# Conv gate and attention on one core: late value groups, early second sigmoids, and the last block's sums on other engines

## The chip, the cores and the metric

One core of a Trainium2 chip runs the whole program. The metric is the device time of one execution in microseconds (us), median of three runs. The core has TensorE (matmuls into PSUM), VectorE, ScalarE, GpSimd (which doesn't reach PSUM here) and SyncE, which issues the DMAs. Each engine works through its own queue in order; semaphores tie the queues together. In the profile they are PE (and PEld for its weight loads), DVE, ACT, POOL and SP.

## The reference

```python
# x: (2, 64, 96, 96); for each of the two images:
h = group_norm1(x, n1_g, n1_b)                    # over the whole image
f = dwconv(h, w3, b3) + dwconv(h, w5, b5) + dwconv(h, w7, b7)
g = sigmoid(conv1x1(f, gate_w, gate_b))
x = x + conv1x1(f * g, proj_w, proj_b)
h = group_norm1(x, n2_g, n2_b)
q, k, v = 1x1 convolutions of h, as (N=9216, 64), (64, N), (N, 64)
attn = softmax(q @ k / 8)                          # 9216 x 9216
out = x + (attn @ v) as an image
```

## The kernel before

**Tiling.** An image's 64 channels x 9216 pixels lie as 128 partitions (two halves of the image) x 4608 columns, in 9 chunks of 512 columns (`CH`). Attention runs in 18 blocks (`NBLK`) of 512 queries; a block visits 36 pairs (`NPAIR`) of key groups of 128. For each pair TensorE makes the scores (`scores`, L969), ScalarE takes the exponential into one of 8 slots of `E` (L538), GpSimd adds one half of it to `accA` (`add_a`, L468) and VectorE the other half to a PSUM bank (`add_b`, L792), and TensorE multiplies it with the values into the accumulation bank (`weigh`, L978). In between TensorE and VectorE look for the row maxima of the next block (`max_scores`, L985, and `reduce_max`, L776). The maxima, once complete, are combined (`maxima`, L783), widened by ScalarE (`widen_maxima`, L561), spread by TensorE (`spread_maxima`, L994) and placed by ScalarE among the queries (`place_maxima`, L567). From the fourth pair on, every odd pair has its scores "seeded": ScalarE copies the maxima into the banks first (`seed`, L574).

**A block's end.** VectorE copies its half of the row sums out of PSUM (`sums_out`, L799), GpSimd adds both parts to `accS` (`total`, L482), TensorE sums over partitions with a matrix of ones (`row_sums`, L1001), ScalarE copies these (`copy_row_sums`, L554), VectorE takes 8 reciprocals of 32 columns (`reciprocals`, L808). The value sums come out of PSUM in four copies (`move_pv`, L547), are added (L501 on GpSimd, or `sum_pv`, L820, on VectorE), multiplied with the reciprocals (L505 or `normalize`, L825), and `write_out` (L833) adds bias and residual. For 17 of an image's 18 blocks this happens during the next block. For an image's last block it is done at once: ScalarE moves all value sums and the row sums right after its last exponential, VectorE takes reciprocals, sum, normalization and write-out right after `sums_out`.

**The seam between the images.** For each of the 9 chunks of the next image TensorE makes the gate product (L1113), ScalarE the sigmoid into `gs` (L628), GpSimd multiplies it with `f` (L511), TensorE makes the projection (L1128), VectorE adds it to x (L891) and takes statistics (`x1_stats`, L883). TensorE issues gate 0, gate 1, the row sums of the last block, and then for each chunk c gate c+2 and projection c. `gs` lies in slots 2 and 3 of `E`, so ScalarE waits ahead of the first sigmoid of image 1 until all additions of the last block are done. After chunk 8 come the aggregate (L898) and a chain of small operations, and SP issues the block's output stores (L400) and, later, the first queries.

**The start of an image's attention.** The list `ITEMS` has 27 entries: 18 chunks of q and k (products L1172, evacuated twice by ScalarE at L653 and L655, with the low part on GpSimd, L521), then 9 groups of values (8 matmul records each, L1163, evacuated at L646). The items use three PSUM banks in turn. From the fourth item on (`LOOK = 3`) the 36 looks (`NVIS`) for block 0's maxima are placed between them: `looks_after(i)` says which looks follow item i, spread evenly over the 24 items left. VectorE reduces each. Then the maxima are widened, spread and placed, and block 0 starts.

Of the kernel before, what the change touches and what calls it, by code (L numbers as in the profile page):

```python
# [9 lines left out]
ALU = mybir.AluOpType  # L10
# [54 lines left out]
def program(nc, x, x_rows, conv_w, per_row, per_channel, matrices, matrices_t, out):  # L65
    with ExitStack() as ctx:
# [96 lines left out]

        ps = ctx.enter_context(nc.psum_tensor("ps", [P, 8, CH], F32))
        S_BANK, MX_BANK, ACC_BANK, SUM_BANK = 0, 4, 6, 7
        STAT_BANK = 3
        STAT1_BANK = (7, 3)
        PROJ_BANK = 2
# [83 lines left out]

        ITEMS = QK_CHUNKS + [(2, g) for g in range(NCH)]
        LOOK = 3
        ITEM_BANK = (2, 3, 6)
        FIRST_MX = (0, 4)

        def looks_after(i):
            each = len(ITEMS) - LOOK
            return range(max(0, i - LOOK) * NVIS // each, max(0, i + 1 - LOOK) * NVIS // each)  # L260

# [165 lines left out]
        def _(pool):  # L429
# [77 lines left out]
            for b in range(B):  # L507
                for c in range(NCH):
                    pool.wait_ge(sig_ready, NCH * b + c + 1)
                    at = f[:, c * CH:(c + 1) * CH]  # L510
                    nc.gpsimd.tensor_tensor(at, at, gs[:, c % 3, :], ALU.mult).then_inc(fg_ready, 1)  # L511
                pool.wait_ge(spread_ready, b + 1)
                nc.gpsimd.partition_all_reduce(reach[:], spread[:], P, RMAX).then_inc(reach_ready, 1)

                for c, (which, chunk) in enumerate(QK_CHUNKS):
                    n = 2 * NCH * b + c
                    cols = slice(chunk * CH, (chunk + 1) * CH)
                    hi, lo = ((QH, QL), (KH, KL))[which]
                    pool.wait_ge(t_ready, n + 1)
                    pool.wait_ge(hi_ready, n + 1)  # L520
                    nc.gpsimd.tensor_tensor(lo[:, cols], T[:, c % 4, :], hi[:, cols], ALU.subtract).then_inc(lo_ready, 1)  # L521
                for j in range(NBLK):
                    attend(b, j)
                total(blk(b, NBLK - 1))


        @block.scalar
        def _(act):
# [89 lines left out]
            for b in range(B):  # L618
                if b:

                    act.wait_ge(adda_free, NSLOT + pair0(b, 0))
                    act.wait_ge(addb_free, NSLOT + pair0(b, 0))
                for c in range(NCH):
                    n = NCH * b + c
                    act.wait_ge(gate_ready, n + 1)
                    if c >= 3:
                        act.wait_ge(fg_ready, n - 2)
                    nc.scalar.activation(gs[:, c % 3, :], ps[:, c % 2, :], ACT.Sigmoid,  # L628
                                         bias=prm[:, GB:GB + 1]).then_inc(sig_ready, 1)
                if b == 0:  # L630
                    act.wait_ge(conv_ps, BESIDE + 1)
                    act.wait_ge(f_out[BESIDE % 2], 16 * COLS * (BESIDE // 2))
                    nc.scalar.activation(evac[:, BESIDE % 2, :, :], ps[:, 4:8, 0:WN], ACT.Copy).then_inc(conv_out, 1)
# [7 lines left out]
                act.wait_ge(scale_ready, b + 1)  # L641
                for i, (which, chunk) in enumerate(ITEMS):
                    bank = ITEM_BANK[i % 3]
                    if which == 2:
                        act.wait_ge(v_ps, NCH * b + chunk + 1)
                        nc.scalar.activation(vals[:, chunk * CH:(chunk + 1) * CH], ps[:, bank, :], ACT.Copy).then_inc(v_out, 1)  # L646
                    else:
# [3 lines left out]
                        if n >= 4:  # L651
# [2 lines left out]
                                             bias=plus, scale=by).then_inc(hi_ready, 1)  # L654
                        nc.scalar.activation(T[:, i % 4, :], ps[:, bank, :], ACT.Identity,  # L655
                                             bias=plus, scale=by).then_inc(t_ready, 1)
                widen_maxima(blk(b, 0))
                place_maxima(blk(b, 0))
                for j in range(NBLK):
                    attend(b, j)  # L660
                move_pv(blk(b, NBLK - 1))
                copy_row_sums(blk(b, NBLK - 1), MX_BANK + 1)


        @block.vector
        def _(dve):
# [211 lines left out]
            for b in range(B):  # L878
# [6 lines left out]
                for c in range(NCH):  # L885
                    n = NCH * b + c
                    dve.wait_ge(proj_ready, n + 1)
                    if c == 0:
                        dve.wait_ge(x_ready, 32 * (b + 1))
                    at = x1[:, c * CH:(c + 1) * CH]  # L890
                    nc.vector.scalar_tensor_tensor(out=at, in0=ps[:, PROJ_BANK + c % 2, :], scalar=prm[:, PB:PB + 1],  # L891
                                                   in1=xs[:, c * CH:(c + 1) * CH], op0=ALU.add,
                                                   op1=ALU.add).then_inc(x1_ready, 1)
                    if c:
                        x1_stats(c - 1)
                x1_stats(NCH - 1)
                dve.wait_ge(bn_done, NCH * (b + 1))
                nc.vector.bn_aggr(mv[:], flat(bn[:])).then_inc(st_in, 1)  # L898
# [34 lines left out]
                maxima(blk(b, 0))  # L933
                for j in range(NBLK):
                    attend(b, j)
                n = blk(b, NBLK - 1)
                for k in range(RECS):
                    reciprocals(n, k)
                sum_pv(n)
                normalize(n)  # L940
                write_out(b, NBLK - 1)


        @block.tensor
        def _(pe):
# [43 lines left out]
            def spread_maxima(n):  # L989

                pe.wait_ge(nm_ready, n + 1)
                for q in range(NQT):
                    for h in (0, 1):
                        a = nc.tensor.matmul(ps[C * h:C * h + C, S_BANK, q * P:(q + 1) * P], negm[:, q, 0:C], ident16[:],  # L994
                                             start=True, stop=True)
                a.then_inc(mb_ready, 1)

            def row_sums(n, bank):
                pe.wait_ge(sum_ready, n + 1)
# [106 lines left out]
            for b in range(B):  # L1106
# [80 lines left out]
                attend(b, NCH - 2, 1)  # L1187
                attend(b, NCH - 1, 0, looks=1)
                attend(b, NCH - 1, 1, looks=0)
            row_sums(B * NBLK - 1, MX_BANK + 1)  # L1190


# [45 lines left out]
```

## Time and profile before

| | us |
|---|---|
| median of three runs | 2831.35 (2830.12 to 2832.53) |
| the profiled execution | 2830.9 |
| its span in the trace | 2828.9 |
| PE busy | 2763.1 (98%) |
| DVE busy | 2503.6 (89%) |
| ACT busy | 2208.5 (78%) |
| POOL busy | 1823.9 (64%) |

The difference between execution and span, 2.0 us, lies around the traced work. Image 0's attention runs from about 164 to 1453 us of the span, image 1's from about 1531 to 2820. A busy share is an average over the stages; at the seam, at the start of an attention and at the end of the program the shares are lower than these. Times in rows are in us from the span's start.

### The profile page before, as it was taken

What the parts mean: (1) busy time and instruction counts of PE and PEld (TensorE: products, weight loads), DVE (VectorE), ACT (ScalarE), POOL (GpSimd) and SP (SyncE); (2) the same over time, 40 slices, a digit from 0 to 9 for tenths busy, and PEclk for the clock granted to TensorE, in tenths of its full rate; (3) what the DMA queues carried; (4) which work ended last, traced back from release to release, by engine and by line L of the source; (5) the groups of instructions that cost most, each with busy time, mean ns of one, the idle gap of its engine ahead of it and who ended that gap; (6) DMA issues with size and microseconds to landing.
All of it is one profiled execution on the core that took longest, in us unless ns stands there. A gap on an engine that the chain in (4) does not pass through costs nothing.

```text
span 2828.9 us, 54483 instructions
## 1 busy us (share of the span) xinstructions
PE 2763.1 (98%) x19644; PEld 935.7 (33%) x19644; DVE 2503.6 (89%) x3172; ACT 2208.5 (78%) x2291; POOL 1823.9 (64%) x1479
## 2 busy tenths in 40 slices
PE   7889999999999999999988999999999999999998
PEld 4233333333333333333323333333333333333332
DVE  5589999999999999999758999999999999999984
ACT  4467888888888888888866788888888888888887
POOL 1446666666666666666754666666666666666666
PEclk9999999999999999999999999999999999999999
DMA  6103000000000000000000000000000000000000
GB/s 203 40 9 75 10 11 10 11 10 10 11 10 11 10 11 11 10 11 9 5 5 16 9 10 11 10 11 11 11 10 10 11 10 11 11 10 11 9 5 5
DMA packets 35768, 48.20 MB, mean 17 GB/s; under 512 B 7848, under 2 KB 33960, under 8 KB 34992
## 3 DMA queue, kind: packets, MB, share of 16 engines
q1 hardware_dynamic: 35504, 44.75, 6.0%
q8 instruction: 157, 2.57, 0.4%
q14 instruction: 107, 0.88, 0.1%
HBM read 16.41 MB, written 9.44 MB: 9 GB/s over the span
## 4 chain that ended last, share of the span: by engine, by line
PE 93%; DVE 4%; issue 1%; ACT 1%; POOL 0%; SPq 0%; DMA 0%; POOLq 0%; DVEq 0%; ACTq 0%
PE ps L978 42%; PE ps L969 35%; PE ps L985 12%; DVE mxp L776 3%; PE ps L1086 2%; PE ps L1113 1%; PE ps L1001 1%; PE ps L1128 0%; DVE ps L792 0%; PE ps L1172 0%; PE ps L1062 0%; PE ps L994 0%; ACT arena L538 0%; DVE bn L883 0%; ACT ps L574 0%
## 5 line engine op out<-in xcount | busy, mean ns | idle before, releaser
L468 POOL TENSOR_TENSOR arena<-arena 128x512 f32<-128x512 f32 x1224 | 1558.8, 1273 | 792.6 <-ACT arena L538 713.7
L776 DVE TENSOR_REDUCE mxp<-ps 128x1 f32<-128x1024 f32 x1296 | 1575.7, 1220 | 174.5 <-PE ps L985 142.6
L538 ACT ACTIVATE arena<-ps,bnd 128x1024 f32<-128x1024 f32 x1296 | 1373.0, 1110 | 422.0 <-PE ps L969 371.7
L978 PE MATMUL ps<-arena,vals 128*64 128x512 f32 x5184 | 1268.2, 605 | 0.2
L969 PE MATMUL ps<-arena 64*128 64x512 f16 x7776 | 1055.1, 377 | 4.1 <-ACT ps L574 2.3
L792 DVE TENSOR_TENSOR ps<-ps,arena 128x512 f32<-128x512 f32 x1224 | 844.8, 690 | 68.1 <-ACT arena L538 67.3
L574 ACT ACTIVATE ps<-mseed 128x1024 f32<-128x1024 f32 x612 | 629.0, 1028 | 53.1 <-ACT arena L538 0.4
L969 PEld LDWEIGHTS ps<-arena 64*128 64x128 f16 x7776 | 376.5, 94 | 419.8 <-ACT arena L538 27.6
L985 PE MATMUL ps<-arena,QM 64*128 64x512 f16 x2592 | 500.6, 383 | 14.1 <-DVE mxp L776 9.6
L978 PEld LDWEIGHTS ps<-arena,vals 128*64 128x64 f32 x5184 | 310.8, 136 | 501.6 <-issue 337.9
L985 PEld LDWEIGHTS ps<-arena,QM 64*128 64x128 f16 x2592 | 124.7, 93 | 734.1 <-DVE mxp L776 632.4
L969 PE MATMUL ps<-arena,one 64*128 64x512 f16 x1368 | 260.9, 378 | 0.0
L808 DVE RECIPROCAL rec<-rsum 128x32 f32<-128x32 f32 x288 | 96.9, 340 | 6.6 <-ACT rsum L554 6.5
L969 PEld LDWEIGHTS ps<-arena,one 64*128 64x128 f16 x1368 | 67.0, 94 | 81.6 <-issue 1.2
L487 POOL TENSOR_SCALAR mseed<-arena 128x512 f32<-128x512 f16 x36 | 53.6, 1490 | 37.3 <-ACT arena L567 34.4
L473 POOL TENSOR_TENSOR arena<-arena 128x512 f32<-128x512 f32 x36 | 45.9, 1275 | 37.8 <-ACT arena L538 37.8
L1086 PE MATMUL ps<-arena 32*24 32x384 f32 x1792 | 54.5, 529 | 13.6 <-issue 7.6
L521 POOL TENSOR_TENSOR arena<-arena 128x512 f16<-128x512 f32 x36 | 41.4, 1159 | 31.8 <-ACT arena L655 31.8
L1172 PE MATMUL ps<-f,wT 128*128 128x512 f32 x72 | 42.4, 685 | 4.9 <-ACT f L639 3.2
L628 ACT ACTIVATE arena<-ps,prm 128x512 f32<-128x512 f32 x18 | 12.3, 687 | 44.6 <-PE ps L1113 44.6
L482 POOL TENSOR_TENSOR accS<-arena 128x512 f32<-128x512 f32 x36 | 46.6, 1295 | 0.2
L511 POOL TENSOR_TENSOR f<-f,arena 128x512 f32<-128x512 f32 x18 | 23.1, 1287 | 36.3 <-ACT arena L628 36.3
(116 smaller groups left out, 668.8 us busy)
## 6 DMA issues: line engine op xcount, KB each, us to landing
arena<-arena SPq DMA_DIRECT2D x144, 64.0 KB, 2.0
arena<-in_x_rows SPq DMA_DIRECT2D x8, 816.0 KB, 10.2
xs<-in_x SPq DMA_DIRECT2D x4, 1152.0 KB, 16.3
f_scratch<-arena SPq DMA_DIRECT2D x32, 144.0 KB
f<-f_scratch SPq DMA_DIRECT2D x16, 288.0 KB, 9.5
QM<-arena SPq DMA_DIRECT2D x72, 64.0 KB, 2.0
xst<-arena SPq DMA_DIRECT2D x72, 64.0 KB, 1.9
out<-ot SPq DMA_DIRECT2D x72, 64.0 KB, 2.0
```

The lines of the kernel that those rows point to most:

```text
L468: nc.gpsimd.tensor_tensor(accA[:, n % 2, :], accA[:, n % 2, :], e, ALU.add).then_inc(adda_free, 1)
L482: nc.gpsimd.tensor_tensor(accS[:], accA[:, n % 2, :], accB[:], ALU.add).then_inc(sum_ready, 1)
L487: nc.gpsimd.tensor_scalar(mseed[:, n % 2, :], QS[:, n % 2, 2, :], ONE * C, None, ALU.mult).then_inc(mseed_ready, 1)
L538: nc.scalar.activation(flat(E[:, slot_of(n % 2, p), :, :]), flat(ps[:, S_BANK + 2 * buf:S_BANK + 2 * buf + 2, :]), ACT.Exp, scale=bnd[:, 6 ...
L574: nc.scalar.activation(ps[:, S_BANK + 2:S_BANK + 4, :], mseed[:, n % 2, :].unsqueeze(1).to_broadcast([P, 2, CH]), ACT.Copy).then_inc(seede ...
L776: nc.vector.reduce_max(flat(mxp[:])[:, v:v + 1], flat(ps[:, bank:bank + 2, :]), AX.X).then_inc(mx_free, 1)
L792: nc.vector.tensor_tensor(ps[:, SUM_BANK, :], ps[:, SUM_BANK, :], e, ALU.add).then_inc(addb_free, 1)
L808: nc.vector.reciprocal(rec[:, at], rsum[:, at]).then_inc(rec_ready, 1)
L969: a = nc.tensor.matmul(ps[:, S_BANK + 2 * (p % 2) + t, :], of[rows], QS[rows, par, part, :], start=(k == 0 and seeds is None), stop=(k == ...
L978: a = nc.tensor.matmul(ps[C * t:C * t + C, ACC_BANK, :], V[:, p, t, :], E[:, slot_of(par, p), t, :], start=(p == 0), stop=(p == NPAIR - 1) ...
L985: a = nc.tensor.matmul(ps[:, bank + t, :], QM[rows, half, qt * P:(qt + 1) * P], KH[rows, kc * CH:(kc + 1) * CH], start=True, stop=True)
L1086: a = nc.tensor.matmul(ps[GRP * h:GRP * h + WROWS, conv_bank(s) + g, 0:WN].rearrange("p (w x) -> p w x", x=W), bands[rows, k * KW + dx, :] ...
```

## The change

It has three parts.

1. **Late value groups.** `looks_after` spreads the 36 looks over items 3 to 24 instead of 3 to 26. The last two value groups come after the last look, with none behind them (`LATE = 2`). ScalarE widens the maxima before it evacuates the last value group, not after it. This is done in both images.
2. **Early second sigmoids.** In image 1, ScalarE waits ahead of the first sigmoid only for the additions up to the last four pairs (`GS_PAIRS`), whose slots `gs` doesn't use. The copies of the last block of image 0 move in between the sigmoids: two value-sum copies each after chunks 1 and 2, the row-sum copy after chunk 3. On VectorE its reciprocals move behind chunks 4 and 5, sum and normalization behind chunk 6, the write-out behind chunk 7.
3. **The program's last block.** GpSimd no longer adds `accA` and `accB`; TensorE sums both over partitions into the same PSUM columns (`row_sums_of_parts`). VectorE takes one reciprocal of 256 columns straight from PSUM; ScalarE's copy goes. GpSimd adds the value sums instead of VectorE.

```diff
@@ looks @@
+        LATE = 2
         def looks_after(i):
-            each = len(ITEMS) - LOOK
-            return range(max(0, i - LOOK) * NVIS // each, max(0, i + 1 - LOOK) * NVIS // each)
+            each = len(ITEMS) - LOOK - LATE
+            return range(min(max(0, i - LOOK), each) * NVIS // each, min(max(0, i + 1 - LOOK), each) * NVIS // each)
@@ gpsimd, after an image's blocks @@
-                total(blk(b, NBLK - 1))
+                n = blk(b, NBLK - 1)
+                if b + 1 < B:
+                    total(n)
+                else:
+                    pool.wait_ge(acc_free, 4 * (n + 1))
+                    pool.wait_ge(o_ready, n + 1)
+                    nc.gpsimd.tensor_tensor(pvt[:], pva[:], pvb[:], ALU.add).then_inc(pv_summed, 1)
@@ scalar @@
-                    act.wait_ge(adda_free, NSLOT + pair0(b, 0))
-                    act.wait_ge(addb_free, NSLOT + pair0(b, 0))
+                    act.wait_ge(adda_free, NSLOT + pair0(b, 0) - GS_PAIRS)
+                    act.wait_ge(addb_free, NSLOT + pair0(b, 0) - GS_PAIRS)
                 for c in range(NCH):
...
+                    if b and c in (1, 2):
+                        move_pv(blk(b, 0) - 1, ((c - 1, 0), (c - 1, 1)))
+                    if b and c == 3:
+                        copy_row_sums(blk(b, 0) - 1, MX_BANK + 1)
...
                 for i, (which, chunk) in enumerate(ITEMS):
                     bank = ITEM_BANK[i % 3]
+                    if i == len(ITEMS) - 1:
+                        widen_maxima(blk(b, 0))
...
-                widen_maxima(blk(b, 0))
                 place_maxima(blk(b, 0))
                 for j in range(NBLK):
                     attend(b, j)
-                move_pv(blk(b, NBLK - 1))
-                copy_row_sums(blk(b, NBLK - 1), MX_BANK + 1)
+                if b + 1 == B:
+                    move_pv(blk(b, NBLK - 1))
@@ vector @@
+                    if b and c in (4, 5):
+                        for k in range(RECS // 2 * (c - 4), RECS // 2 * (c - 3)):
+                            reciprocals(blk(b, 0) - 1, k)
+                    if b and c == 6:
+                        sum_pv(blk(b, 0) - 1)
+                        normalize(blk(b, 0) - 1)
+                    if b and c == 7:
+                        write_out(b - 1, NBLK - 1)
...
-                n = blk(b, NBLK - 1)
-                for k in range(RECS):
-                    reciprocals(n, k)
-                sum_pv(n)
-                normalize(n)
-                write_out(b, NBLK - 1)
+            n = blk(B - 1, NBLK - 1)
+            dve.wait_ge(rs_ready, n + 1)
+            dve.wait_ge(norm_done, n)
+            nc.vector.reciprocal(rec[:], ps[:, MX_BANK + 1, 0:HCH]).then_inc(rec_ready, RECS)
+            normalize(n)
+            write_out(B - 1, NBLK - 1)
@@ tensor @@
+            def row_sums_of_parts(n, bank):
+                pe.wait_ge(accb_out, n + 1)
+                for h in (0, 1):
+                    nc.tensor.matmul(ps[C * h:C * h + C, bank, 0:HCH], ones[:, 0:C],
+                                     accB[:, h * HCH:(h + 1) * HCH], start=True, stop=False)
+                pe.wait_ge(adda_free, NSLOT + NPAIR * (n + 1))
+                for h in (0, 1):
+                    a = nc.tensor.matmul(ps[C * h:C * h + C, bank, 0:HCH], ones[:, 0:C],
+                                         accA[:, n % 2, h * HCH:(h + 1) * HCH], start=False, stop=True)
+                a.then_inc(rs_ready, 1)
...
-            row_sums(B * NBLK - 1, MX_BANK + 1)
+            row_sums_of_parts(B * NBLK - 1, MX_BANK + 1)
```

## Rows read from the trace of the kernel before

**Rows 1.** The page, part 4: the chain that ended last, shares by engine.
```profile
PE 93%; DVE 4%; issue 1%; ACT 1%; POOL 0%; SPq 0%; DMA 0%; POOLq 0%; DVEq 0%; ACTq 0%
```

**Rows 2.** By stretches: length, busy us (count) of five engines, granted clock, DMA.
```profile
1458.40:1462.00 3.60, 3.58 (x5) 1.46 (x6) 2.85 (x3) 1.23 (x2) 3.51 (x3) 0.53 0.00 0
1510.00:1528.00 18.00, 16.25 (x106) 10.47 (x104) 17.99 (x17) 7.44 (x12) 2.82 (x3) 1.00 0.06 15
1528.00:1534.00 6.00, 3.07 (x22) 1.40 (x24) 1.29 (x2) 3.19 (x4) 1.54 (x1) 0.69 0.17 44
```

**Rows 3.** Timeline, seam: start, duration, engine, line, operation, [idle before <-releaser].
```profile
1453.37 1.98 PE L1113 MATMUL ps<-f,wT 128*128 128x512 f32 x4
...
1455.29 0.65 PE L1001 MATMUL ps<-accS,ones 128*64 128x256 f32 x4
...
1458.67 1.32 DVE L825 TENSOR_TENSOR pvt<-pvt,rec 128x256 f32<-128x256 f32 x1
...
1463.65 1.02 PE L1113 MATMUL ps<-f,wT 128*128 128x512 f32 x2
...
1465.48 1.26 POOL L511 TENSOR_TENSOR f<-f,arena 128x512 f32<-128x512 f32 x1 [0.44 <-ACT arena L628]
...
1469.01 0.75 DVE L891 SCALAR_TENSOR_TENSOR arena<-ps,prm,xs 128x512 f32<-128x512 f32 x1 [0.36 <-PE ps L1128]
...
1470.52 1.02 PE L1113 MATMUL ps<-f,wT 128*128 128x512 f32 x2
...
1473.71 0.73 DVE L891 SCALAR_TENSOR_TENSOR arena<-ps,prm,xs 128x512 f32<-128x512 f32 x1
...
1474.96 0.73 DVE L891 SCALAR_TENSOR_TENSOR arena<-ps,prm,xs 128x512 f32<-128x512 f32 x1
...
1476.92 0.40 DVE L898 BATCH_NORM_AGGREGATE mv<-bn 128x2 f32<-128x54 f32 x1
```

**Rows 4.** Timelines of DVE, PE and ACT, start of image 1's attention.
```profile
1487.89 41.21 DVE L776 TENSOR_REDUCE mxp<-ps 128x1 f32<-128x1024 f32 x36 [2.99 <-PE ps L985]
...
1525.22 1.16 PE L1163 MATMUL ps<-wT,f 128*128 128x128 f32 x8
...
1529.36 0.63 ACT L561 ACTIVATE negm<-m 128x512 f16<-128x512 f32 x1 [2.35 <-DVE m L783]
...
1530.04 0.45 PE L994 MATMUL ps<-ident,negm 128*64 128x128 f16 x8 [2.86 <-ACT negm L561]
...
1531.15 1.28 ACT L538 ACT_TABLE_LOAD   x1
...
1535.02 1.11 ACT L538 ACTIVATE arena<-ps,bnd 128x1024 f32<-128x1024 f32 x1 [0.59 <-PE ps L969]
...
1536.22 1.03 ACT L574 ACTIVATE ps<-mseed 128x1024 f32<-128x1024 f32 x1
...
1537.40 0.82 PE L969 MATMUL ps<-arena 64*128 64x512 f16 x6 [0.28 <-ACT ps L574]
```

**Rows 5.** Timelines of ACT and PE, start of image 0's attention.
```profile
163.80 0.60 ACT L567 ACTIVATE arena<-ps 128x512 f16<-128x512 f32 x1 [0.51 <-PE ps L994]
...
170.41 0.82 PE L969 MATMUL ps<-arena 64*128 64x512 f16 x6 [1.09 <-ACT ps L574]
```

**Rows 6.** Timeline of the program's tail.
```profile
2816.78 3.65 PE L978 MATMUL ps<-arena,vals 128*64 128x512 f32 x16
...
2821.28 0.78 ACT L547 ACTIVATE pvb<-ps 64x256 f32<-64x256 f32 x2
...
2822.69 1.83 DVE L808 RECIPROCAL rec<-rsum 128x32 f32<-128x32 f32 x8 [2.87 <-ACT rsum L554]
...
2824.91 0.43 DVE L825 TENSOR_TENSOR pvt<-pvt,rec 128x256 f32<-128x256 f32 x1
2825.37 0.48 DVE L833 SCALAR_TENSOR_TENSOR ot<-pvt,prm,xst 128x256 f32<-128x256 f32 x1
```

**Rows 7.** Instructions of L501: count, duration in ns (min/median/max), first and last start.
```profile
L501 POOL TENSOR_TENSOR pvt<-pva,pvb x34: 723/730/742, 269.4 to 2779.6; 128x256 f32<-128x256 f32 x34
```

More of the change, by code:

```diff
@@ L165, in program @@
         S_BANK, MX_BANK, ACC_BANK, SUM_BANK = 0, 4, 6, 7
+        GS_PAIRS = 4
         STAT_BANK = 3
```

## The prediction

> **What bounds the kernel now.** I first read the chain that ended last. TensorE holds 93% of it [rows 1], and in the attention blocks TensorE runs without gaps, so nothing of this change that lies beside those blocks counts. The change touches three other places, which I then read in the timeline and in the view by stretches: the seam between image 0 and image 1, the start of the first attention block of each image, and the tail after the last block. In all three TensorE waits for a serial chain through other engines. Twice the granted clock then falls to half: 0.53 in the seam's first sigmoid chunks and 0.69 on average around the start of block 0 [rows 2].
>
> **Seam, what sets its length.** Before, ScalarE moves the value sums, waits for the row sums, copies them, loads the sigmoid table and only then starts chunk 0. Afterwards TensorE paces the chunks: gate matmuls 4 and 8 start at 1463.65 and 1470.52, so one chunk (a gate and a projection product) takes 6.87 / 4 = 1.72 us [rows 3]. VectorE ends the stage: the last x1 chunk starts at 1474.96 and the aggregate of the statistics at 1476.92 [rows 3]. That aggregate is my marker.
>
> **Seam, the change.** The wait on the last four pairs goes. Those pairs use other slots of E than the sigmoid results, and the awaited additions are done while the block still runs. The table load has to follow the last exponential. I take it that it runs ahead of the gate wait, as the exponential's load does: it starts at 1531.15, when the scores it serves aren't there yet (TensorE makes them from the placed maxima, which are finished just then) [rows 4]. Gate 0 starts at 1453.37. A gate's start is followed by its product on GpSimd 1.83 us later (1463.65 to 1465.48), which takes 1.26 [rows 3], so product 0 is ready at 1456.46. On TensorE the four row-sum passes end at 1455.29 + 0.65 = 1455.94 [rows 3]. Gate 2 follows there, and projection 0 at 1456.80, so GpSimd is in time and TensorE has no gap in which the clock falls. Gate 8 then starts at 1455.94 + 6 x 1.72 = 1466.25 instead of 1470.52: **4.27 us** earlier. Of this 1.8 is the half-clock stretch.
>
> VectorE cannot follow. Its eight reciprocals, sum, normalize and write-out stood ahead of chunk 0, in time when it had nothing else; now they stand in chunks 4 to 7, where it has 1.72 - 1.25 = 0.47 spare per chunk (1.25 from chunk 7 at 1473.71 to chunk 8 at 1474.96 [rows 3]). From chunk 4 on it is the bound. Chunk 4 started at 1469.01 [rows 3], now at 1464.74. From there come four pairs of 1.25, the last chunk's 1.96 up to the aggregate, and the moved work. The same work at the tail, with GpSimd idle, takes from 2822.69 to 2825.37 + 0.48, or 3.16 us [rows 6]. The aggregate starts at 1464.74 + 5.00 + 1.96 + 3.16 = 1474.86 against 1476.92: a gain of **2.1 us**. Half of the 4.27 is given back, since the cover is gone. ScalarE's four copies (0.39 each) and the row-sum copy fit into its slack between sigmoids. The stores of the last block are issued later by SP; it queues the first queries of image 1 behind them, but these wait for a q chunk that comes ten us after either write-out. Cost nothing. Bounds: +0.8 if the table load stood behind the gate wait (1.3 later), and -0.6 if sum, normalize and write-out all took what normalize takes beside busy GpSimd (1.32 instead of 0.43 [rows 3, 6], some 0.9 more for each of the three). I take 2.1, since the last product on GpSimd ends near 1469.4 and the sum comes only at about 1470.3.
>
> **Start of block 0.** 36 reductions run back to back on VectorE for 41.21 us up to 1529.10 [rows 4]. Spreading the looks over 22 instead of 24 items cannot shorten that, and TensorE keeps up: it is busy for 16.25 of 18 us of that stretch, VectorE for 17.99 [rows 2], and two items leave it. What changes is what TensorE does at the end. It has been idle for 2.86 us before the maxima are spread at 1530.04 [rows 4], so from 1527.18, and the clock falls. Now two value groups (1.16 each [rows 4]) stand there and end at 1529.5, before the widened maxima arrive at 1529.99 (1529.36 + 0.63). The waits that remain are 0.5 us there and some 0.9 for the placed maxima. The drop followed a wait of 2.86 us, so I take it that with these the clock stays. On ScalarE one eviction of 0.60 now stands between widening and placing; it fills a wait for TensorE and delays placing by 0.1. It also queues behind ScalarE's wait for the maxima, and only the first scores, which wait for the placing anyway, wait for it.
>
> With the full clock the chain from the placed maxima to the first seeded pass of scores belongs to ScalarE: load 1.30, two exponentials of 1.11, a gap of 0.09, the seed of 1.03, and 0.15 to TensorE, or 4.79 us [rows 4]. A warm pass (0.82 for six matmuls [rows 4]) hides in the load and in the exponential. Before, it was 1537.40 - 1531.13 = 6.27 in image 1 and 170.41 - 164.40 = 6.01 in image 0 [rows 5]. The gains are 1.48 and 1.22, less 0.1 each: **2.5 us**. Bounds: -0.2 (the clock falls all the same) and +2.8.
>
> **Tail.** Before, VectorE's part goes over GpSimd's total, four row-sum passes, ScalarE's copy, eight reciprocals and the sum to normalize at 2824.91 [rows 6]. Now the passes over accB and accA follow the last value matmul at 2816.78 + 3.65 = 2820.43; both parts are ready by then. Eight passes cost at most twice the 0.65 of four [rows 3], I take until 2821.6. One reciprocal of 256 columns isn't in the trace: bounds are 0.43 (normalize, of the same shape) and 1.83 (the eight, whose columns these are) [rows 6]; I take 1.5, near the eight, as it is their operation and only their starts are saved. Normalize can begin at 2821.6 + 0.05 + 1.5 + 0.05 = 2823.2. GpSimd's value sum starts when ScalarE's moves end at 2821.28 + 0.78 = 2822.06, takes 0.73 and is over at about 2822.9 [rows 6, 7]: hidden. Gain **1.7 us**, bounds 1.25 (2821.73 and 1.83) and 2.0 (GpSimd's sum is then last).
>
> By the Trainium skill, "VectorE: DVE Perf Modes", "First, the fixed hardware budget", the reciprocal is an iterative divide with a repeat count of 8; read as eight cycles per column at its 0.96 GHz that is an estimate of 2.13 us for 256 columns, a tail gain near 0.9 and a whole gain near 5.5. The trace is against this reading: the eight together need 1.83 with all their starts.
>
> **The sum.** 2.5 + 2.1 + 1.7 = 6.3 us. The profiled execution took 2830.9 (span 2828.9, 2.0 around it), 0.45 under the median of 2831.35; it becomes 2824.6, and the median 2825.05, so **2825.1**.
>
> **The rivals.**
> - The clock falls at block 0 although the value groups fill the wait, since two waits and the short spread still leave TensorE half idle there. For it: the drop before followed 2.86 us of waiting; against it: the new waits are under 1. Block 0 gives -0.2, the sum is 3.6, the time 2827.7. Chance 0.2.
> - VectorE's moved work meets GpSimd's products. Then the seam gives -0.6, the sum is 3.6 and the time 2827.7. For it: normalize took 1.32 beside them [rows 3]; against it: by then the products should have ended. Chance 0.12. The Trainium skill, "SBUF — State Buffer", "SBUF: two separate sides", says that a VectorE operation with two SBUF inputs and a GpSimd operation exclude each other for a whole instruction; the 1.32 agrees.
> - The sigmoids don't start early, because the table load stands behind the gate wait: the seam gives 0.8, the time is 2826.4. Chance 0.08.
> - The reciprocal is dearer than its eight parts (by the rule above the tail gives 0.9): 2825.9. Chance 0.06.
> - **Slower**: with value groups taken out from between the looks, TensorE idles more while VectorE reduces, and the clock falls already there. The two late groups then run at half speed, 2 x 2.2 = 4.4 us, to 1531.6, the spread (0.9) ends 2.0 later than before, in both images, and the start stays cold. It decides from the point where the groups end after 1530.0. Block 0 costs 4.0; with the seam's bad end (-0.6) and the tail's 1.7 the sum is 2.9 slower, 2834.2. Against it: without two groups (2.3 us) TensorE still works for some 14 of the 18 us [rows 2]. Chance 0.04.
>
> **How the numbers follow.** The forecast has 0.5, between 2823.0 and 2826.8. To hold 8 in 10, the range reaches to the two rivals at 2827.7 and their spread: 2823.0 to 2828.3. A difference of 0.2% (5.7 us, so a time under 2825.7) is about what a measurement of this kernel can tell. The forecast is only 0.6 from that border: of its 0.5 about 0.42 is beyond it, and the dearer reciprocal and the good ends of the rivals add 0.08. The slower rival's time is within 0.2% of now; only its far part is beyond. Faster 0.5, same 0.48, slower 0.02.
>
> **What would show it.** Seam: first sigmoid near 1454.4, no clock below 1.0 from 1453 to 1470, VectorE without gaps from chunk 4, aggregate near 1474.9. Block 0: the reductions still end within 0.2 us of 1529.1 less the seam's gain; 4.8 to 4.9 us from placed maxima to the seeded scores, at full clock. Tail: normalize 2.8 us after the last value matmul instead of 4.5, one reciprocal of 1.5. The forecast is wrong if the clock falls at 1530, if the moved work takes over 4 us, or if an attention block changes its pace.

## The result and the profile after

The changed kernel takes 2824.27 us (median of 14 runs, 2822.21 to 2826.88) against 2830.28 (14 runs, 2828.25 to 2832.53) of the kernel before in the same comparison: 6.0 us less, ratio 0.9979 with a 95% interval of 0.9972 to 0.9986 (a gain between 4.0 and 7.9 us). Forecast were 6.3 us less and a time of 2825.1. The profiled execution took 2825.39 with a span of 2823.7, 5.2 under the span of before.

The page of the changed kernel, busy shares and chain by engine:

```profile
span 2823.7 us, 54475 instructions
PE 2759.1 (98%) x19648; PEld 935.0 (33%) x19648; DVE 2501.6 (89%) x3164; ACT 2207.9 (78%) x2290; POOL 1823.3 (65%) x1479
PE 93%; DVE 4%; issue 1%; ACT 1%; POOL 0%; SPq 0%; DMA 0%; DVEq 0%; ACTq 0%; POOLq 0%
```

Neither the shares nor the chain [rows 1] show where 5 us went; they are spread over three places. So I cut both traces at the same instructions and compare the stretches. The numbers are differences of times in the timelines. "Gate 0" is the start of image 1's first gate product, "aggregate" that of the x1 statistics' aggregate, "first reduction" VectorE's first reduction of a look, "m4" the instruction that combines the maxima (L783), "placed" the end of `place_maxima` and "seeded" the start of the first scores on seeded banks:

| stretch (us) | before | after | gain |
|---|---|---|---|
| start to image 0's aggregate (not touched) | 105.84 | 105.17 | 0.67 |
| image 0: first reduction to m4 | 42.50 | 42.37 | 0.13 |
| image 0: placed maxima to first seeded scores | 6.01 | 4.71 | 1.30 |
| image 0: from there to gate 0 (attention) | 1282.96 | 1282.95 | 0 |
| seam: gate 0 to aggregate | 23.55 | 22.49 | 1.06 |
| seam: aggregate to first reduction | 10.97 | 12.24 | -1.27 |
| image 1: first reduction to m4 | 41.24 | 41.12 | 0.12 |
| image 1: placed maxima to first seeded scores | 6.27 | 4.72 | 1.55 |
| image 1: from there to the last value matmul's end | 1283.03 | 1283.00 | 0 |
| tail: from there to normalize | 4.48 | 2.88 | 1.60 |

The stretches not listed are the same within 0.05. Part 1 gives 3.1 us here, part 3 1.6, part 2 nothing (1.06 - 1.27 = -0.2), and 0.67 lies ahead of all changes, where this stretch took 102.1 to 106.1 in the executions profiled for this study.

**Seam.** The changed kernel's timeline, which answers to [rows 3] (start, duration, engine, line, operation, [idle before <-releaser]):

```profile
1451.28 1.98 PE L1148 MATMUL ps<-f,wT 128*128 128x512 f32 x4
...
1452.51 1.28 ACT L638 ACT_TABLE_LOAD   x1 [3.23 <-PE ps L1148]
1453.19 0.65 PE L1036 MATMUL ps<-accS,ones 128*64 128x256 f32 x4
1453.80 1.26 ACT L638 ACTIVATE arena<-ps,prm 128x512 f32<-128x512 f32 x2
1454.54 1.12 PE L1148 MATMUL ps<-f,wT 128*128 128x512 f32 x2 [0.70 <-ACT arena L638]
...
1463.92 0.75 DVE L906 SCALAR_TENSOR_TENSOR arena<-ps,prm,xs 128x512 f32<-128x512 f32 x1 [0.36 <-PE ps L1163]
...
1465.18 0.97 DVE L823 RECIPROCAL rec<-rsum 128x32 f32<-128x32 f32 x4
...
1468.93 1.10 PE L1163 MATMUL ps<-f,wT 128*128 128x512 f32 x2 [0.76 <-DVE arena L906]
1469.30 0.41 DVE L835 TENSOR_TENSOR pvt<-pva,pvb 128x256 f32<-128x256 f32 x1
...
1473.77 0.40 DVE L921 BATCH_NORM_AGGREGATE mv<-bn 128x2 f32<-128x54 f32 x1
```

The second line is the surprise. ScalarE is idle for 3.23 us and loads the table only when gate 0 is there; TensorE then waits 0.70 us for the sigmoid ahead of gate 2, up to 1454.54. From chunk 4 (1463.92) on VectorE has no gap, and TensorE waits for it ahead of the last projection (0.76). From 1453 to 1470 the clock stays at full, where it was 0.53 in the first chunks before [rows 2]. But it falls afterwards. By stretches (length, busy us and count of PE, PEld, DVE, ACT, POOL, granted clock, DMA share, GB/s):

```profile
1453.00:1470.00 17.00, 15.33 (x37) 6.03 (x36) 10.79 (x23) 9.81 (x16) 11.35 (x9) 1.00 0.00 1
1471.00:1484.00 13.00, 6.21 (x10) 3.19 (x11) 9.09 (x33) 4.62 (x8) 1.53 (x2) 0.51 0.08 20
1527.00:1534.00 7.00, 4.03 (x39) 1.70 (x39) 2.72 (x4) 6.48 (x9) 2.80 (x2) 1.00 0.11 28
```

It falls during TensorE's wait for the statistics. The first statistics product of the kernel before, and behind it that of the changed kernel:

```profile
1477.38 0.38 PE L951 MATMUL ps<-mv,ones 128*128 128x2 f32 x2 [2.59 <-DVE mv L898]
1474.22 0.59 PE L974 MATMUL ps<-mv,ones 128*128 128x2 f32 x2 [4.20 <-DVE mv L921]
```

In the kernel before the wait was 2.59 us and this product still ran at full clock; the clock fell only behind it (0.57 from 1478 to 1486). In the changed kernel the wait is 4.20 us and the product takes 0.59 instead of 0.38.

**Start of block 0** (1527 to 1534, last line): clock 1.00, where it was 0.69 [rows 2]. TensorE's timeline there, which answers to [rows 4]:

```profile
1525.21 2.05 PE L1198 MATMUL ps<-wT,f 128*128 128x128 f32 x16
1528.04 0.41 PE L1017 MATMUL ps<-ident,negm 128*64 128x128 f16 x8 [0.77 <-ACT negm L570]
1529.35 0.82 PE L992 MATMUL ps<-arena 64*128 64x512 f16 x6 [0.89 <-ACT arena L576]
...
1533.81 0.82 PE L992 MATMUL ps<-arena 64*128 64x512 f16 x6 [1.18 <-ACT ps L583]
```

and ScalarE's:

```profile
1527.36 0.63 ACT L570 ACTIVATE negm<-m 128x512 f16<-128x512 f32 x1 [0.35 <-DVE m L798]
1527.89 0.58 ACT L662 ACTIVATE vals<-ps 128x512 f32<-128x512 f32 x1
1528.49 0.60 ACT L576 ACTIVATE arena<-ps 128x512 f16<-128x512 f32 x1
```

The two value groups (16 records) stand in the former wait of 2.86 us; waits of 0.77 and 0.89 are left. The extra eviction (L662) ends just as the spread does.

**Tail**, which answers to [rows 6]:

```profile
2816.65 0.60 PE L1025 MATMUL ps<-arena,ones 128*64 128x256 f32 x4
...
2817.08 0.60 PE L1029 MATMUL ps<-arena,ones 128*64 128x256 f32 x4
...
2817.89 1.76 DVE L962 RECIPROCAL rec<-ps 128x256 f32<-128x256 f32 x1 [1.69 <-PE ps L1029]
2818.52 0.72 POOL L533 TENSOR_TENSOR pvt<-pva,pvb 128x256 f32<-128x256 f32 x1 [2.02 <-ACT pvb L556]
2819.69 0.42 DVE L840 TENSOR_TENSOR pvt<-pvt,rec 128x256 f32<-128x256 f32 x1
```

### The profile page after: what moved, and what is told of

The parts are those of the page before. It is cut to its first block, busy times and chain, and to the rows that moved or that the text cites. A ratio compares the mean times of both kernels' runs of the same rounds, so it can differ in the third digit from the quotient of the medians.

```text
span 2823.7 us, 54475 instructions
## 1 busy us (share of the span) xinstructions
PE 2759.1 (98%) x19648; PEld 935.0 (33%) x19648; DVE 2501.6 (89%) x3164; ACT 2207.9 (78%) x2290; POOL 1823.3 (65%) x1479
## 4 chain that ended last, share of the span: by engine, by line
PE 93%; DVE 4%; issue 1%; ACT 1%; POOL 0%; SPq 0%; DMA 0%; DVEq 0%; ACTq 0%; POOLq 0%
PE ps L1001 42%; PE ps L992 35%; PE ps L1008 12%; DVE mxp L791 3%; PE ps L1121 2%; PE ps L1036 1%; PE ps L1207 0%; PE ps L1148 0%; PE ps L1163 0%; DVE ps L807 0%; PE ps L1097 0%; PE ps L1017 0%; ACT arena L547 0%; DVE bn L898 0%; ACT ps L583 0%
```

## The experiments

A comparison of times has an interval of about 0.1% here (2.5 us), which can't tell single microseconds apart. So the verdicts rest on the stretches of the table, and the ratios only say whether the whole follows. How far the stretches can be trusted, the kernels with an unchanged seam show (the kernel before and the runs of parts 1 and 3 alone and of the constants ahead of the spread): gate 0 to aggregate took 23.31 to 23.55 in them, aggregate to first reduction 10.82 to 11.02, both together 34.1 to 34.6. Image 0's aggregate to first reduction, which no run changes, took 14.1 or 14.3, and the unchanged start of image 0's block 0 took 6.01 to 6.12. Where the clock stays at full, stretches repeat much better: the attention blocks within 0.06 us (but for one case below), the tail and the starts of block 0 within 0.03, and in the changed kernel and its variants gate 0 to aggregate is 22.49 four times and 21.23 or 21.24 three times. So only where the clock falls is a difference under about 0.4 us not told apart from the spread. The text compares with the profile of the kernel before (23.55 and 10.97). These were the theories. **Theory**: part 1 and the seam's losses are matters of TensorE's clock; part 2 is held back by the table load, then by VectorE. **Rivals** stand in each expectation.

**One part at a time.** Part 1 alone (`looks_after` and the place of `widen_maxima`):

> The kernel before with part 1 alone (late value groups, maxima widened ahead of the last one). My theory: the gain is TensorE's clock. The two value groups fill its wait of 2.86 us, the granted clock stays at full, and from the end of the last block-0 reduction to the first seeded scores it takes 6.7 us instead of 8.0 (image 0) and 8.3 (image 1); the whole gains 2.4 to 3.0 us (ratio 0.9990 to 0.9991). Rival: the reordering of the looks itself shortens the 36 reductions; then their 41.2 us shrink and the time behind them stays at 8.0 and 8.3.

Ratio 0.9990 (0.9981 to 0.9999). From placed maxima to the seeded scores 4.71 and 4.72, and the reductions 0.15 and 0.12 shorter; all else as before within the spread above. The theory holds, and the sum is 3.1 us of the trace; the rival has those 0.12 to 0.15 per image and no more.

Part 2 alone (the changes to sigmoids, copies and VectorE's seam work, with row sums, reciprocals and value sums at the tail as before):

> The kernel before with part 2 alone (early second sigmoids, the copies, reciprocals and write-out of the last block of image 0 moved in between). My theory: from gate 0 to the aggregate 22.5 us instead of 23.55, since the sigmoid table is loaded only once gate 0 is there, but TensorE then idles 4.2 instead of 2.6 us ahead of the statistics and its clock falls earlier, so from the aggregate to the first look's reduction it takes 11 to 12.3 us instead of 10.97: net -0.3 to 1.1 us, ratio 0.9996 to 1.0001. Rival (the forecast): 2.1 us stay, ratio 0.9993.

Ratio 1.0000 (0.9991 to 1.0009). Gate 0 to aggregate 22.49, aggregate to first reduction 11.37: net 0.66 in the trace. The forecast's 2.1 are not there. (This expectation was written with the changed kernel's profile known, the forecast without it.)

Part 3 alone:

> The kernel before with part 3 alone (TensorE adds both row-sum parts, one reciprocal out of PSUM, GpSimd adds the value sums). My theory: from the last value matmul's end to normalize 2.9 us instead of 4.5, one reciprocal of 1.76: gain 1.6 us, ratio 0.9994. Rival: the rows of the changed kernel mislead because the other parts shift the tail; then this run shows another interval than 2.9.

Ratio 0.9991 (0.9982 to 1.0000). Last value matmul to normalize 2.87, as in the changed kernel.

**The table load.** One instruction and one tile more than the changed kernel:

```diff
                     act.wait_ge(addb_free, NSLOT + pair0(b, 0) - GS_PAIRS)
+                    nc.scalar.activation(early[:], ones[:, 0:1], ACT.Sigmoid)
```

> The changed kernel with one more instruction: a sigmoid of one column of constants right after the last exponential of image 0, which carries the waits on the additions, so that the table is loaded there. Theory: the wait on gate 0 had been put on the table load; now the first sigmoid starts 1.1 us after gate 0 instead of 2.5, projection 0 comes at 3.4 to 3.6 after gate 0 instead of 4.6, and the aggregate 1.1 to 1.3 us earlier, at 21.2 to 21.4 after gate 0. Whether it reaches the end depends on the clock behind the aggregate: 0 to 1.3 us under the changed kernel, ratio 0.9974 to 0.9979. Rival: VectorE alone sets the seam; then the aggregate stays at 22.5.

ScalarE's timeline of this run:

```profile
1449.22 1.28 ACT L634 ACT_TABLE_LOAD   x1
1450.52 0.20 ACT L634 ACTIVATE early<-ones 128x1 f32<-128x1 f32 x1
1452.37 0.69 ACT L640 ACTIVATE arena<-ps,prm 128x512 f32<-128x512 f32 x1 [1.65 <-PE ps L1150]
```

The load follows the last exponential, the sigmoid starts 1.16 after gate 0 instead of 2.52, and the aggregate comes at 21.23 instead of 22.49: 1.26 us, nearly the whole delay of the sigmoid (1.36). Gate 8 starts 12.90 after gate 0 instead of 14.15. Ratio 0.9977 (0.9968 to 0.9986).

Why did it wait? In the list of ScalarE's instructions each wait is attached to one of them. In the changed kernel and, below it, in the next one (lines of that list, not of a view; the waits of the traced instructions agree for the changed kernel):

```
L638 ACT_TABLE_LOAD [waits gate_ready,addb_free]
L638 ACTIVATE arena<-ps,prm 128x512 [waits adda_free]
...
L640 ACT_TABLE_LOAD [waits addb_free,adda_free]
L640 ACTIVATE arena<-ps,prm 128x512 [waits gate_ready] x2
```

Here the wait that the source names first stays with the function, the others go to the load ahead of it. It is the same with the exponential's load in the kernel before: its source names the wait on the scores first, and that one stays with the exponential. The next run only changes which is named first:

```diff
+                    act.wait_ge(gate_ready, NCH * b + 1)
                     act.wait_ge(adda_free, NSLOT + pair0(b, 0) - GS_PAIRS)
                     act.wait_ge(addb_free, NSLOT + pair0(b, 0) - GS_PAIRS)
...
-                    act.wait_ge(gate_ready, n + 1)
+                    if c or not b:
+                        act.wait_ge(gate_ready, n + 1)
```

> The changed kernel with one line moved: the wait on gate 0 is written ahead of the two waits on the additions, not behind them. In the order of ScalarE's instructions the gate wait then sits on the sigmoid and the waits on the additions on the table load (in the changed kernel the gate wait sits on the load). Theory: nothing but that placement cost the 1.3 us; first sigmoid 1.16 us after gate 0 as with the extra instruction, aggregate at 21.23. Rival: an extra instruction is needed since a load waits for all that its function waits for; then 2.52 and 22.49 stay.

```profile
1449.49 1.28 ACT L640 ACT_TABLE_LOAD   x1
1452.63 0.69 ACT L640 ACTIVATE arena<-ps,prm 128x512 f32<-128x512 f32 x1 [1.86 <-PE ps L1150]
```

1.16 to the first sigmoid, 21.24 to the aggregate; ratio 0.9976 (0.9967 to 0.9986). The order in which three waits are written was worth 1.26 us of the seam up to the aggregate. The times of the whole don't show it: the changed kernel itself has 0.9979 and, once more below, 0.9976.

**The clock behind the aggregate.** Constants on TensorE in the changed kernel:

```diff
+            def keep_clock(k, bank=MX_BANK):
+                for _ in range(k):
+                    nc.tensor.matmul(ps[:, bank, 0:P], ones[:], ident[:], start=True, stop=True)
...
-                    stats(2 * (B + b), ones)
+                    keep_clock(13)
+                    stats(2 * (B + b), ones, between=lambda: keep_clock(1))
+                    keep_clock(9)
```

> The changed kernel with 23 matmuls of constants on TensorE (128x128, into a PSUM bank nobody reads): 13 behind the last projection, 1 between the two statistics products, 9 behind them. They give nothing but a busy TensorE. Theory: what the early aggregate lost came from the clock; with it kept at full, aggregate to first item product takes 4.8 instead of 5.2 us, item product to first reduction 5.9 to 6.2 instead of up to 7.05, so 1.3 to 1.6 us less than in the changed kernel's profile, on average over runs about 0.8 (ratio 0.9976). It can't go under some 10.9 from aggregate to reduction, since the query transfer sets it then. Rival: the 12.24 come from something else that moved (ScalarE's or SP's queue); then they stay.

TensorE's timeline in the changed kernel:

```profile
1478.96 6.61 PE L1207 MATMUL ps<-f,wT 128*128 128x512 f32 x8 [2.92 <-ACT f L653]
1485.50 0.39 PE L1008 MATMUL ps<-arena,QM 64*128 64x512 f16 x2
```

and with the constants:

```profile
1473.01 0.38 PE L974 MATMUL ps<-mv,ones 128*128 128x2 f32 x2 [1.30 <-DVE mv L921]
...
1477.33 2.81 PE L1213 MATMUL ps<-f,wT 128*128 128x512 f32 x6 [0.80 <-ACT f L653]
1480.42 1.12 PE L1213 MATMUL ps<-f,wT 128*128 128x512 f32 x2 [0.28 <-ACT arena L671]
1482.32 0.39 PE L1008 MATMUL ps<-arena,QM 64*128 64x512 f16 x2 [0.77 <-DMA QM<-arena]
```

In the changed kernel the clock is 0.50 up to about 1484.9, and the four products ahead of the first look are one block of 6.61 us which the look has to follow; with the constants it is 1.00 from 1468 to 1483, the products are done early, and the look waits for its queries' transfer. Aggregate to first reduction 10.26 instead of 12.24. It even went under the floor of 10.9 that I had set from the transfer: the queries too come from an item product, which is now earlier. It is also less than the 10.97 of the kernel before, whose clock fell behind the statistics too. The rival, that something else had moved, is out. Ratio 0.9976 (0.9966 to 0.9986), again no lower than the changed kernel's.

> The changed kernel once more, for what its seam does in another execution. Theory: the stretch from aggregate to first reduction depends on when TensorE's clock comes back, and differs from one execution to the next: between 11.0 and 12.3 us, while gate 0 to aggregate stays at 22.49. Rival: 12.24 is what the early aggregate costs each time.

Gate 0 to aggregate 22.49 again, but aggregate to first reduction 11.21. The statistics products still ran at half clock (0.59 instead of 0.38, aggregate to first item 5.19 as in the profile above), but the clock came back sooner, at about 1481.6 (8.5 us behind the aggregate; 11.1 in the profile of the first section). So 0.4 us is lost up to the first item product each time. The total depends on the execution: aggregate to first reduction took 11.21 here, 11.57 in the wait-order run, 11.23 with the early load and 11.37 with part 2 alone, 0.2 to 0.6 over the 10.97 of the kernel before. The 12.24 of the first section is the worst of five. What sets when the clock comes back, no run shows. Ratio 0.9976 (0.9967 to 0.9985).

**Is part 1 only the clock?** The kernel before, with constants in place of late groups:

```diff
+                keep_clock(8, SUM_BANK)
                 spread_maxima(blk(b, 0))
```

> The kernel before with 8 matmuls of constants on TensorE between the last look and the spread of the maxima, in both images; value groups and looks stand where they stood. Theory: part 1 works by the clock alone; then from the end of the reductions to placed 2.0 us as before, from placed to the first seeded scores 4.7 instead of 6.0 and 6.3, a gain of 2.9, as much as part 1 (ratio 0.9990). Rival: it is the order of the value groups, or ScalarE's order; then 6.0 and 6.3 stay.

```profile
1523.89 2.05 PE L1000 MATMUL ps<-ident,ones 128*128 128x128 f32 x16
1526.82 0.41 PE L994 MATMUL ps<-ident,negm 128*64 128x128 f16 x8 [0.88 <-ACT negm L561]
```

4.71 and 4.72 from placed to seeded, reductions 42.49 and 41.25 as before; ratio 0.9992 (0.9983 to 1.0002). Eight useless matmuls do what two value groups do, up to the 0.12 to 0.15 per image of shorter reductions.

**Can VectorE's work go elsewhere?** The early load, and reciprocals, sum, normalize and write-out moved behind `normalize_x1(H_ACT + H_DVE, NCH)`, where VectorE waits for the first look. The cut shows VectorE's new part; the store on SyncE, a wait of VectorE and one of TensorE move with it:

```diff
+                if b:
+                    for k in range(RECS):
+                        reciprocals(blk(b, 0) - 1, k)
+                    sum_pv(blk(b, 0) - 1)
+                    normalize(blk(b, 0) - 1)
+                    write_out(b - 1, NBLK - 1)
```

> The changed kernel with the sigmoid table loaded early (as in the run of that name) and VectorE's reciprocals, sum, normalize and write-out of image 0's last block moved from chunks 4 to 7 to the time in which VectorE waits for the first look (after its last part of the normalized x1); SP stores that block behind the first queries, TensorE waits for the copies out of PSUM instead of the write-out. Theory: VectorE was the bound of the seam from chunk 4 on; the aggregate comes 1.8 to 2.0 us earlier than with the early load alone, at 19.3 us after gate 0, and the moved 3 us hide in the 3.9 us wait, so the first reduction isn't later for it. Whole: 1.9 us under the early load (ratio 0.9970). Rival: the moved work delays the first look's reduction by more than it saves, ratio 0.9977 or above.

```profile
1471.91 0.40 DVE L921 BATCH_NORM_AGGREGATE mv<-bn 128x2 f32<-128x54 f32 x1
...
1479.87 1.83 DVE L828 RECIPROCAL rec<-rsum 128x32 f32<-128x32 f32 x8
...
1482.54 1.30 DVE L853 SCALAR_TENSOR_TENSOR ot<-pvt,prm,xst 128x256 f32<-128x256 f32 x1
1483.76 9.13 DVE L796 TENSOR_REDUCE mxp<-ps 128x1 f32<-128x1024 f32 x8
```

The aggregate comes at 19.30 after gate 0, as worked out: VectorE was the bound. But TensorE starts the first look's scores at 1482.30, which a free VectorE would reduce 0.50 us later (1487.39 and 1487.89 in the kernel before), and VectorE reduces them at 1483.76, since the moved work is in the way; the write-out took 1.30 beside GpSimd instead of 0.47. Aggregate to reduction 11.85. Of the 1.94 us up to the aggregate 1.31 are left at the first reduction (31.15 after gate 0 against 32.46 with the early load alone). Image 1's attention took 1283.36 instead of 1283.0, here and in the next run; the 0.36 are lost at one place, the start of block 15 (at 2611), where TensorE waits for a reduction, and the cause is open. So about 0.9 us is kept in the trace. The theory's 1.9 is not there, and neither does the work delay the reduction by more than it saves, as the rival has it. Ratio 0.9981 (0.9972 to 0.9990), which can't decide between them.

> The same with 17 matmuls of constants that keep TensorE busy behind the last projection (7), between the statistics products (1) and behind them (9). Theory: aggregate at 19.3 after gate 0, then 10.9 to the first reduction, in every run; ratio 0.9968. Rival: the shorter wait alone keeps the clock as in the kernel before, and the constants change nothing.

19.30, then 12.61: with the clock kept, the first look is ready even sooner, and normalize (1.29) and write-out (1.26) both meet GpSimd. Ratio 0.9977 (0.9967 to 0.9986). Both expectations miss: the constants change something, for the worse (31.91 against 31.15 from gate 0 to the first reduction). This place doesn't hold 3 us.

**Both gains together, without moving the work:** early load and `keep_clock` with 9, 1 and 9.

> The changed kernel with the sigmoid table loaded early and 19 matmuls of constants that keep TensorE busy around the statistics. Theory: both gains of the seam add, gate 0 to aggregate 21.2, aggregate to first reduction 10.3; 2.2 to 3.2 us under the changed kernel's 34.7 for both, ratio 0.9968 to 0.9971. Rival: one hides the other; the sum stays at 32.5 or more.

21.24 and 10.47, sum 31.71 against 34.73 in the changed kernel's profile and 33.70 in its second; ratio 0.9973 (0.9963 to 0.9984), a little above the 0.9968 to 0.9971 expected. In the stretches they add, though nine constants didn't hold the clock all the time: the last 18 records took 3.80 us, 2.25 at full clock, and delayed the first item product by half a microsecond.

**The moved work in portions.** As the last, with 7, 1 and 9 constants:

```diff
@@ scalar, ahead of the first sigmoid @@
+                    move_pv(blk(b, 0) - 1, ((0, 0), (0, 1)))
@@ scalar, behind chunk c @@
+                    if b and c == 1:
+                        move_pv(blk(b, 0) - 1, ((1, 0), (1, 1)))
+                    if b and c == 2:
+                        copy_row_sums(blk(b, 0) - 1, MX_BANK + 1)
@@ vector, behind chunk c @@
+                    if b and c == 1:
+                        sum_pv(blk(b, 0) - 1)
+                    if b and c in (2, 3, 4):
+                        for k in range(3 * (c - 2), min(RECS, 3 * (c - 1))):
+                            reciprocals(blk(b, 0) - 1, k)
+                    if b and c == 5:
+                        normalize(blk(b, 0) - 1)
+                    if b and c == 6:
+                        write_out(b - 1, NBLK - 1)
```

> As the run before it, and the moved work is spread to fit each chunk's 0.47 us of slack: two value-sum copies ahead of the first sigmoid, two after chunk 1, the row-sum copy after chunk 2; on VectorE the sum behind chunk 1, three reciprocals behind chunks 2 and 3, two behind 4, normalize behind 5, write-out behind 6. Theory: VectorE's 3.2 us were the bound only because they stood in chunks 4 to 7; spread they cost about 0.4, gate 0 to aggregate 19.7, then 10.3: sum 30.0, ratio 0.9964. Rival: they meet GpSimd's products and push the chunks; then the aggregate stays above 20.7.

```profile
1450.93 1.99 PE L1156 MATMUL ps<-f,wT 128*128 128x512 f32 x4
...
1458.44 0.41 DVE L838 TENSOR_TENSOR pvt<-pva,pvb 128x256 f32<-128x256 f32 x1
...
1465.47 0.41 DVE L843 TENSOR_TENSOR pvt<-pvt,rec 128x256 f32<-128x256 f32 x1
...
1470.67 0.40 DVE L925 BATCH_NORM_AGGREGATE mv<-bn 128x2 f32<-128x54 f32 x1
...
1480.94 41.09 DVE L794 TENSOR_REDUCE mxp<-ps 128x1 f32<-128x1024 f32 x36 [2.30 <-PE ps L1012]
```

19.74 and 10.27, sum 30.01. Median 2820.61 (6 runs) against 2830.88, ratio 0.9966 (0.9954 to 0.9978): the shortest seam of the study and the lowest median, some 3 us under the changed kernel by the medians; the intervals of the two overlap, the stretches don't (30.0 against 33.7 and 34.7). The same 3.2 us of VectorE cost 1.94 in chunks 4 to 7 (21.24 against 19.30 without them) and 0.44 (19.74) when they are cut to the slack. The sum and normalize start in GpSimd's gaps between two products and the write-out behind its last (0.41, 0.41 and 0.47).

## Why the prediction was right, and where it was not

The total was right (6.3 against 6.0), and so was the remark that it lies at the 0.2% border. That it came so close is in part luck: of its three terms one was 0.6 too small and one 1.3 to 2.3 too large. The terms as measured in the profiles add up to 4.5 to 5.5 us, which the interval of 4.0 to 7.9 holds as well.

- **Start of block 0**, 2.5 forecast, 3.1 measured. The mechanism is as forecast: the clock stays, and the chain ScalarE takes over, worked out as 4.79, took 4.71. The delay of 0.1 for the extra eviction didn't come: it ends with the spread. The reductions took 0.12 to 0.15 less in each image, against "cannot shorten that". In image 1, 0.09 of the 0.12 is one place: before, the last look but one started at 1526.31, behind a value group, and VectorE's reductions were 1.22 apart there instead of 1.13; that group is now late. The constants show that the clock does the rest.
- **Seam, TensorE's pace**: 4.27 forecast up to gate 8; in the changed kernel it is 3.0 (1465.43 - 1451.28 = 14.15 against 17.15). The step that failed is "I take it that it runs ahead of the gate wait, as the exponential's load does". The rival with chance 0.08 was right, with its price of 1.3. The exponential's load had run early because its own waits, on additions and value matmuls, were met; that says nothing of where another function's waits land. With the load early the pace was as forecast: gate 8 came at 12.90 after gate 0, 4.25 less than before.
- **Seam, VectorE's bound**: right. Chunk 4 to aggregate took 9.85 where 10.12 was worked out and 7.91 was before, so 1.9 us of the gain are given back there, and the runs with an early load gave 2.3 up to the aggregate where 2.1 was forecast. Sum and normalize came after GpSimd's last product and took 0.41 and 0.43; the rival of a meeting there was wrong for the chunks, and right for the later place in the experiments (1.30).
- **Seam, behind the aggregate**: this term was missing. I treated what follows the aggregate as unchanged, but an earlier last projection and VectorE's longer work leave TensorE idle 4.20 us instead of 2.59 ahead of the first statistics product, and it then runs at half clock. That gives back 0.2 to 1.3 us. The seam's net is 0.7 to 0.8 in two executions (part 2 alone, and the changed kernel once more) and -0.2 in one, instead of 2.1; the unchanged seam itself varies by 0.4.
- **Tail**, 1.7 forecast, 1.60 measured. One reciprocal of 256 columns took 1.76, taken as 1.5, near its upper bound of 1.83; the eight passes were faster than taken (start of the reciprocal 1.08 after the last value matmul, forecast 1.22). GpSimd's sum is hidden, as forecast. The paragraph on the divide has a slip: with 2.13 for the reciprocal the sum written there gives a tail gain of 1.1 (0.9 only with the later end of the passes). The measured 1.76 is between 1.5 and 2.13, and under the eight parts' 1.83.
- **Clock in the look stretch** (the slower rival): wrong. The clock is 1.00 from 1485 to 1527, and the two late groups took 2.05, not 4.4.

What stays open: when the clock comes back behind the statistics; the 0.36 us in block 15 of the runs with moved work; and the time ahead of image 0's aggregate varies by 4 us between executions, as much as the effects here, which I followed no further.

## What to carry to other kernels

An engine's idle time is not free where its clock depends on it: here needed work, or even useless matmuls, in TensorE's wait of 2.86 us made the serial chain behind the wait 1.3 to 1.55 us shorter, and a change that drew a wait out from 2.59 to 4.20 us made the chain behind it 0.2 to 1.3 us longer. Work that is moved off a chain needs slack in each step it is put into, and not only in their sum: the same 3.2 us cost 1.9 in four chunks and 0.4 in six. When a function needs a new table, look at which wait lands on the load; in this kernel the order in which the waits are written decided it.

## What the runs showed of the hardware

- A reciprocal costs about 6.3 ns per column: 1.76 us for 256 against 0.16 to 0.17 for one or two columns. One long instruction saves almost nothing over eight of 32 (1.83). The Trainium skill, "VectorE: DVE Perf Modes", "First, the fixed hardware budget", gives a repeat count of 8; at its 0.96 GHz the measured slope is six cycles, an estimate. It lies under the eight; a multiplication of the same 256 columns took 0.42 us, under two such cycles per column.
- A table load takes 1.28 us, and the next function starts 0.02 us behind it (load 1449.22, function 1450.52). The Trainium skill, "ScalarE: Activation LUTs", "What ACT_TABLE_LOAD costs", gives 1283 ns, which agrees, and adds a drain of 1.38 us per switch, which this trace doesn't show, behind the load or ahead of it: the exponential before it ended at 1449.21.
- Normalize and write-out, with two inputs in SBUF, took 1.26 to 1.32 us beside GpSimd's operations and 0.41 to 0.48 in their gaps: 1.32 in the seam of the kernel before and 0.43 at its tail [rows 3, 6], 1.29 and 1.26 in the run with moved work and constants.
